# Value spreads cut in halves, three turns of positions moved into a loop, and one key spread moved two steps, in an eight-layer kernel

## What is computed

```python
pe = pos_emb.reshape(Sq, Sq, NH, DH)
k_hop = jnp.einsum('bhvc,vmhc->bhvm', qh, pe)
qk = jnp.einsum('bhsd,bhtd->bhst', qh, k_scaled)
C = (qk + k_hop) * D
```

## Time and profile before

| | us |
|---|---|
| three runs | 758.37, 757.95, 753.97 |
| median | 757.95 |
| the profiled execution | 758.14 |
| span of its trace | 756.3 |
| busy: PE, PEld, DVE, ACT, POOL | 655.7, 451.2, 572.8, 525.6, 319.4 |
| mean granted clock of TensorE | 0.947 |

### The profile page before, as it was taken

One profiled execution on the slowest core, in us unless ns is written; L12 is line 12 of the kernel. 1 busy time (PEld: TensorE's weight loads), 2 busy tenths in 40 slices (PEclk: granted clock), 3 DMA queues, 4 the chain that ended last, 5 costly groups with the idle time before them and its releaser, 6 DMA issues.

```text
span 756.3 us, 13768 instructions
## 1 busy us (share of the span) xinstructions
PE 655.7 (87%) x5031; PEld 451.2 (60%) x5039; DVE 572.8 (76%) x1105; ACT 525.6 (70%) x1074; POOL 319.4 (42%) x337
## 2 busy tenths in 40 slices
PE   6288999488997998998799999988999998888967
PEld 5167887233554554655795666546888686666622
DVE  5869997887898857998565888668973346666777
ACT  4775663567885764677438776747885689999877
POOL 4776675787766778881000000189930040000000
PEclk8579999799999999999799999989999999999998
DMA  8526482111110114410000000700000000000001
GB/s 301 173 57 181 130 136 70 49 45 35 38 38 25 33 51 76 66 38 12 1 1 1 0 1 1 281 2 1 2 1 1 1 1 1 1 0 1 1 0 55
DMA packets 40273, 36.11 MB, mean 48 GB/s; under 512 B 21800, under 2 KB 30256, under 8 KB 40208
## 3 DMA queue, kind: packets, MB, share of 16 engines
q1 hardware_dynamic: 33616, 21.73, 9.8%
q0 software_dynamic: 6592, 13.51, 7.6%
HBM read 30.11 MB, written 5.11 MB: 47 GB/s over the span
## 4 chain that ended last, share of the span: by engine, by line
PE 57%; DVE 19%; ACT 13%; issue 4%; DMA 3%; POOL 3%; SPq 0%; ACTq 0%; DVEq 0%; POOLq 0%
PE ps L1351 5%; PE ps L1567 4%; PE ps L1604 3%; PE ps L2073 3%; PE ps L1002 3%; PE ps L2337 3%; PE ps L2024 3%; PE ps L1595 3%; PE ps L213 2%; ACT big L2393 2%; PE ps L1585 2%; POOL pe L400 2%; PE ps L217 2%; PE ps L1031 2%; PE ps L1516 2%
## 5 line engine op out<-in xcount | busy, mean ns | idle before, releaser
L1497 POOL DMA_INDIRECT pe<-in_rpe,idx x128 | 135.0, 1055 | 35.7 <-issue 24.5
L1963 POOL TENSOR_SCALAR big<-big,wcols 128x256 f32<-128x256 f32 x1 | 0.9, 937 | 138.9 <-DMA big<-in_l3f_w 138.9
L384 POOL DMA_INDIRECT pe<-normed_rows,pe x46 | 48.6, 1057 | 20.2 <-issue 10.1
L525 ACT ACTIVATE pe<-ps,wcols 128x256 f32<-128x256 f32 x92 | 38.5, 476 | 22.4 <-PE ps L432 22.4
L1707 ACT ACTIVATE big<-ps,small 128x128 f32<-128x128 f32 x128 | 34.7, 382 | 17.5 <-PE ps L1595 17.5
L1212 ACT ACTIVATE big<-ps 128x1024 f32<-128x1024 f32 x32 | 32.6, 1019 | 18.1 <-PE ps L999 17.9
L1351 PE MATMUL ps<-nT,big 128*128 128x512 f16 x192 | 44.5, 379 | 0.0
L432 PE MATMUL ps<-big 128*128 128x256 f16 x276 | 36.8, 287 | 5.6 <-DVE big L578 4.4
L2337 PEld LDWEIGHTS ps<-big,pe 128*128 128x128 f32 x288 | 34.3, 192 | 11.9 <-ACT big L2385 5.9
L1232 DVE TENSOR_REDUCE small<-ps 128x16 f32<-128x1024 f32 x32 | 38.3, 1216 | 1.5 <-PE ps L993 1.5
L2337 PE MATMUL ps<-big,pe 128*128 128x128 f32 x288 | 35.5, 277 | 1.8 <-ACT big L2385 1.8
(11 more groups left out here) (429 smaller groups left out, 1971.2 us busy)
## 6 DMA issues: line engine op xcount, KB each, us to landing
pe<-in_l2f_w SPq DMA_DIRECT2D x16, 256.0 KB, 6.1
tile_results<-big SPq DMA_DIRECT2D x23, 128.0 KB, 2.2
pe<-in_xrow SPq DMA_DIRECT2D x4, 512.0 KB, 5.3
big<-in_l0x_w SPq DMA_DIRECT2D x8, 256.0 KB, 7.0
pe<-in_rpe,idx POOLq DMA_INDIRECT x128
cT<-in_cT SPq DMA_DIRECT2D x2, 512.0 KB, 4.6
nT<-in_l0x_w SPq DMA_DIRECT2D x4, 256.0 KB, 7.7
vx<-in_l0x_w SPq DMA_DIRECT2D x4, 256.0 KB
```

The costliest lines, as they stand in the source:

```text
L384: pool.indirect_dma_start(out=xg16[:, i % RX, h, :, :].rearrange("p r n -> p (r n)"), out_offset=None, in_=xrows_d, in_offset=bass.Indirec ...
L525: ins_ = act.activation(hid32[:, i % RF, f, :], hidden_ps(i, u)[:, f % 2, :], ACT.Relu, bias=wcols[:, bass.ds(at + (COL_AT["l0x_b1"][0] + ...
L1497: pool.indirect_dma_start(out=pe[:, v * D:(v + 1) * D], out_offset=None, in_=ins["rpe"], in_offset=bass.IndirectOffsetOnAxis(ap=idx[:, v:v ...
```

## The change

1. GpSimd's first key spread (batch 13) moves from step 8 to step 6: `KEYS_IN = (6, 9, 10)`.
2. In layer 3 the last step (k = 15) has no turn between selectors and components any more; its three turns come after the components, on TensorE and on Scalar (`between(k)`).
3. Spreads of chunks 1, 2 and 3 are cut into two halves: positions 0 to 63 (u = 0) and 64 to 127 (u = 1) of each batch. Before the hop loop only the first halves are made. The second halves of chunk 1 are GpSimd's, eight instructions behind its last gather (`pool_rest4`). Those of chunks 2 and 3 are made inside the hop loop: two by Vector after each of f = 0, 2, ..., 10, one by Scalar after each of f = 1, 3, 5, 9. TensorE waits for all 24 of them at f = 16.
4. Vector norms chunk 2, spreads its halves, and only then norms chunk 3.
5. Turns 29, 30 and 31 leave the head and go into the hop loop, at f = 7, 11 and 15, on TensorE and on Scalar.

```diff
-        POOL_KEYS, KEYS_IN = range(13, B), (8, 9, 10)
+        POOL_KEYS, KEYS_IN = range(13, B), (6, 9, 10)
...
+        def between(k):
+            return 13 <= k < NC * NCH // 2 - 1
...
-                    if done == "sel" and k >= 13:
+                    if done == "sel" and between(k):
                         pe_turn_positions(te, first_turn(k))
...
-                if k >= 13:
+                if between(k):
                     act_turned(act, first_turn(k))
...
+        def half4(c, h, u):
+            vs = slice(u * S // 2, (u + 1) * S // 2)
+            return (qblk[:, c * BC:(c + 1) * BC, vs, h], nT[:, cs(c)].rearrange("p (b v) -> p b v", b=BC)[:, :, vs],
+                    hm8[:, h:h + 1])
...
+        def dve_half4(dve, c, h, u):
+            dve.tensor_scalar(*half4(c, h, u), None, MUL).then_inc(s_rest4 if u else X4["qblk"], 1)
+
+        def pool_rest4(pool):
+            pool.wait_ge(s_norm, 2 * NCH + 2)
+            for h in range(NH2):
+                pool.tensor_scalar(*half4(1, h, 1), None, MUL).then_inc(s_rest4, 1)
...
+        LATE_TURNS = (7, 11, 15)
...
-            pe_turn_positions(te, PG - 3)
-            pe_turn_positions(te, PG - 2)
             pe_gates4(te, 1)
-            pe_turn_positions(te, PG - 1)
             pe_gates4(te, 2)
             pe_gates4(te, 3)
-            te.wait_ge(X4["peT_act"], PG)
+            te.wait_ge(X4["peT_act"], PG - 3)
             te.wait_ge(X4["qblk"], NH2 * NCH)
             for f in range(PG):
+                if f in LATE_TURNS:
+                    pe_turn_positions(te, PG - 3 + LATE_TURNS.index(f))
+                if f == PG // 2:
+                    te.wait_ge(s_rest4, REST_0 + NH2 * (NCH - 1))
+                if f >= PG - 3:
+                    te.wait_ge(X4["peT_act"], f + 1)
...
-            for g in range(PG - 3, PG):
-                act_turned(act, g)
             for c in (2, 3):
                 act.wait_ge(s_norm, 2 * NCH + c + 1)
                 for h in (6, 7):
-                    act_spread4(act, c, h)
+                    act_half4(act, c, h, 0)
...
+                if f in LATE_TURNS:
+                    act_turned(act, PG - 3 + LATE_TURNS.index(f))
+                if f in (1, 3, 5, 9):
+                    n = (1, 3, 5, 9).index(f)
+                    act_half4(act, 2 + n // 2, 6 + n % 2, 1)
...
             for h in range(NH2):
-                dve_spread4(dve, 1, h)
-            dve_normed(dve, 4, 2, bank(4))
-            dve_normed(dve, 4, 3, bank(5))
+                dve_half4(dve, 1, h, 0)
             for c in (2, 3):
+                dve_normed(dve, 4, c, bank(2 + c))
                 dve.wait_ge(s_norm, 2 * NCH + c + 1)
                 for h in range(6):
-                    dve_spread4(dve, c, h)
+                    dve_half4(dve, c, h, 0)
...
                 dve.tensor_copy(*khop_group(f)).then_inc(X4["khop_dve"], 1)
+                if f < 12:
+                    for n in (f, f + 1):
+                        dve_half4(dve, 2 + n // 6, n % 6, 1)
...
             if stop > 2:
                 pool_layer2(pool, link)
+            if stop > 4:
+                pool_rest4(pool)
```

More of the change, by code:

```diff
@@ L1364, in pe_layer3 @@
                         te.wait_ge(s_norm, 2 * NCH)
-                    for g in range(first_turn(k) + (k >= 13), first_turn(k + 1)):
+                    for g in range(first_turn(k) + between(k), first_turn(k + 1)):
                         pe_turn_positions(te, g)
@@ L1403, in act_turned, with act_half4 @@
             act.activation(*turned(g), ACT.Copy).then_inc(X4["peT_act"], 1)
+        s_rest4, REST_0 = F1["up"], FT * NCH
         def spread4(c, h):
-            return qblk[:, c * BC:(c + 1) * BC, :, h].rearrange("p b v -> p (b v)")
-        def act_spread4(act, c, h):
-            act.activation(spread4(c, h), nT[:, cs(c)], ACT.Copy, scale=hm8[:, h:h + 1]).then_inc(X4["qblk"], 1)
-        def dve_spread4(dve, c, h):
-            dve.tensor_scalar(spread4(c, h), nT[:, cs(c)], hm8[:, h:h + 1], None, MUL).then_inc(X4["qblk"], 1)
+            return qblk[:, c * BC:(c + 1) * BC, :, h].rearrange("p b v -> p (b v)"), nT[:, cs(c)], hm8[:, h:h + 1]
+        def half4(c, h, u):
+            vs = slice(u * S // 2, (u + 1) * S // 2)
+            return (qblk[:, c * BC:(c + 1) * BC, vs, h], nT[:, cs(c)].rearrange("p (b v) -> p b v", b=BC)[:, :, vs],
+                    hm8[:, h:h + 1])
+        def act_spread4(act, c, h):
+            dst, src, mask = spread4(c, h)
+            act.activation(dst, src, ACT.Copy, scale=mask).then_inc(X4["qblk"], 1)
+        def act_half4(act, c, h, u):
+            dst, src, mask = half4(c, h, u)
+            act.activation(dst, src, ACT.Copy, scale=mask).then_inc(s_rest4 if u else X4["qblk"], 1)
+        def dve_spread4(dve, c, h):
+            dve.tensor_scalar(*spread4(c, h), None, MUL).then_inc(X4["qblk"], 1)
+        def dve_half4(dve, c, h, u):
[4 more added lines that the diff above has]
+                pool.tensor_scalar(*half4(1, h, 1), None, MUL).then_inc(s_rest4, 1)
         def dve_layer3(dve, link):
```

## The result

| | before | after |
|---|---|---|
| median of 19 runs, us | 758.09 | 753.03 |
| lowest and highest, us | 753.35 to 760.14 | 747.69 to 755.97 |
| ratio (95% interval) | | 0.9931 (0.9914 to 0.9948) |
| profiled execution, us | 758.14 | 754.47 |
| span of its trace, us | 756.3 | 752.6 |

5.1 us less by the medians, where 4.0 were forecast. The sum was nearly right; its terms were not. Lines of the code have moved: layer 3's products are L1354, turns L1539, full and half spreads of Vector L1427 and L1430, GpSimd's halves L1435, hop products L1594, the first score products behind the loop L1612 (L1585 before), L1443 is L1466, L1448 is L1471.

What follows compares the result with a forecast made beforehand. No engine bounds the whole span; Vector bounds layer 3's head, TensorE the hop loop. Terms -3.4 - 1.9 + 1.3 = -4.0 us against 758.14 gave 754.1, stated as 754.0; 8 in 10 between 749.5 and 759.

Steps and rivals of the forecast that it cites:

- Part 1: Layer 2, key spread in step 6 instead of 8: L1304 freed, taken -3.4 us, bounds -1.2 and -4.7.
- the new meeting: Step 9: batch 14's key spread holds up Vector's L1301, which ends at 240.7 instead of 238.8.
- the late form of part 1: Query spread follows in step 9 without a gap, perhaps low clock; step 10 at 244.0, gain as low as 1.2 us.
- Part 1's reason: Step 9: L1301, issued 0.1 us ahead of the key spread, loses as L1304 did with 0.63 us.
- The new place in step 6: Key spread starts at 220.4, L1301 ends at 220.23: 0.2 us of air, nothing counted, small chance of a 3 us stall.
- Part 2: Layer 3, step 15: four transposes of 0.44 us leave the way of the last components; xT earlier, taken -0.4 us.
- Part 3: Head, spreads by halves at 0.35 us each: loop starts at 364.4 instead of 366.3, -1.9 us including the earlier xT.
- the alternation: Layer 3's end and head: GpSimd's halves and Vector take turns; L1448 waits 0.9 us twice, L1412 0.9 each; chance 0.45.
- The example at 501: L2213, issued at 501.43 inside the first of two 1.16 us GpSimd instructions, ended at 502.51 between them.
- Part 4: Hop loop: three turns on TensorE at 0.44 us each, taken +1.3 us, bounds +1.3 and +1.8.
- The whole stop of Vector: Rival: GpSimd's eight halves in a row hold Vector before the hop loop; total about 758, up to 761.3 us; chance 0.13.
- The second, no new meeting: Rival, step 9: L1301 gets through first, sum -5.3 to -6.9, 751 to 753 us; chance 0.25.

Runs made afterwards that it cites:

- the run without the meeting: Changed kernel with the key spreads in steps 7, 10 and 11 instead of 6, 9 and 10: 749.29 us, ratio 0.9871.
- turns in the wait: Changed kernel with key spreads in steps 7, 10 and 11 and turns 29 and 30 between gate products of chunks 2 and 3: 748.48 us, ratio 0.9849.
- the memset: Changed kernel with a 0.22 us GpSimd memset between the last gather and each of the three key spreads: 748.27 us, ratio 0.9847.
- the run with the turns back: Changed kernel with turns 29 to 31 moved from the hop loop back into the head: 750.23 us, ratio 0.9863.

## Why the prediction was right, and where its terms were not

**Part 1, the gain and the new meeting: right.** Forecast -3.4 up to step 10, measured -3.4. L1301 was to take 2 to 3 us and took 2.58; TensorE was to wait 2 to 3 us before step 10 and waited 2.02. The low clock behind it was left for the late form of part 1; it came in the changed kernel's profile behind 2.02, took 1.6 us, and did not come in the four other profiles on the first two chips with this wait (2.01 three times, 2.02 once). What decides isn't shown. The query spread followed without a gap, as the late form had feared, and cost Vector nothing, because L1301 came in first.

**Part 1's reason: right in its assumption, now with a test.** I took L1301 to lose although it is issued first. It lost with 0.11 us of lead behind a gather, and won with 0.39 and 0.20 behind a memset. The literal reading of the Trainium skill's page "SBUF — State Buffer" ("Who interferes with whom": whoever issues first keeps the ports) would have given -4.7, and the run without the meeting shows what that would have been worth: 1.5 us more. If the hold begins during the gather, the page's sentence and the rows agree again, and the recorded start is not the moment of the issue. That reading fits all meetings here, but where the hold begins isn't measured.

**The new place in step 6: right.** 0.2 us of air was enough. L1301 there has 0.68 us.

**Part 2, -0.4: mis-sized.** The first half of xT is done 0.4 us earlier, as forecast: at 349.37, and layer 3 starts 0.9 us earlier here, so this is 350.3 in the count of the kernel before, which had 350.70. But the step "the three turns then lie in the 2.66 idle us before L213" was costed at nothing, and it is worth more than the 0.44: with turn 26 at 347.71 the idle before L213 is 1.17 us, the clock stays up, and L213 takes 1.96 instead of 3.03 us, the two turns behind it 0.87 instead of 1.48 on the chain. Undone alone, the edit costs 1.5 us up to the loop's start.

**Part 3, -1.9 with part 2: the step that failed is the alternation.** L1448 was to wait twice 0.9 us and L1412 twice; they waited not at all, and GpSimd waited up to 4.3 us for them. The example at 501 was the other case, a Vector instruction that comes while a GpSimd one is running and has gaps before it; Vector's instructions here follow each other with none. The price is 0.6 us in one block of this profile, and nothing in eight others. The prediction's own sum was off here too: the waits that it lists on L1448 and L1412 add up to 3.6 us, and it moved Vector's end of chunk 1 by 2.8 (355.7 to 358.5). With 3.6 parts 2 and 3 would have come to -1.1 and the whole to -3.2. Halves cost 0.29 to 0.30, between the bound of 0.26 and the 0.35 taken, which over the twenty on Vector's way is 1.1 us. Undisturbed I had 362.8 - 366.3 = -3.5 for parts 2 and 3; the marks show -5.2 (77.9 to 72.7 us from layer 3's first product to the loop), and -5.7 in five profiles without the 0.6. The clock of part 2 (1.7) and the cheaper halves make up the difference: Scalar had the norm of chunk 2 ready so early that only 0.2 us of Vector's time was lost waiting for it. The loop's start is then set by the last gate products, at clock 0.50 until 360.20, 0.1 us behind Vector's last half.

**Part 4, +1.3: the turns cost it, the loop doesn't lose it all.** On the chain each turn in the loop has 0.44 us. From the first hop product to the first score products (L1585, now L1612) it takes 34.7 us instead of 34.0: +0.7, since full clock is back 4.5 us after the start (364.7) and not 5.7 us. Vector and Scalar have room: the copies of the first f still end ahead of f+3.

```profile
368.87 0.44 PE ps L1539 x4
369.31 0.89 PE ps L1594 x8
```

**The rivals.** The whole stop of Vector didn't happen. The second, no new meeting, is seen in three experiments on the first two chips (spreads in 7, 10 and 11, turns in the wait, the memset) and is 1.5 us better, or 3.1 where the clock would fall.

**The sum: luck in good part.** The terms as measured are -3.4, -5.2 and +0.7, together -7.9, twice the forecast. In the profiled pair 1.6 us of low clock behind the second meeting, 0.9 ahead of layer 2 and 1.7 in the rest bring this back to -3.7. None of the three stands in the forecast's sum. By the medians 5.1 are left.

## What to carry to other kernels

A GpSimd instruction that reads SBUF must be laid out against Vector's instructions with two SBUF operands, with the gather in front of it counted in: moving it away from one meeting can put it into the next, and a memset of 0.22 us in front of it was as good as a better step on the second chip (layer 2 took 100.8 us either way). It is no cure by itself: in the kernel before, on the third chip, the key spread behind the memset stopped the next Vector instruction instead. Small work of TensorE belongs in its waits, and it isn't enough to take it off the path: two turns put into an idle stretch gave 0.9 us themselves, and the stretch gained 1.4 more with the clock, in one profile. Where an edit saves a few microseconds, compare stretches between marks in the traces, and look whether a stretch without an edit moves with it; the rest, which no edit touches, took 352.4 to 357.8 us here, with the clock.

## What the runs showed of the hardware that I had not expected

- The meeting of GpSimd and Vector goes either way. A key spread behind a gather stopped a Vector instruction issued 0.11 and 0.63 us ahead of it; behind a memset it waited for one issued 0.20 and 0.39 us ahead; a row of Vector instructions without gaps held a GpSimd half for 4.3 us (5.52 instead of 1.17 to 1.20), and did so in seven profiles (5.50 to 5.62). In the two profiles in which the halves were through before that row began, none took over 2.44.
- Spreads with a distance of eight elements in the output: on GpSimd 256 elements take 1.17 us where a plain 128x256 took 0.94. On Vector 256 take 0.29 and 512 take 0.51 us, on Scalar some 0.6 (1.25 for two) and 1.03.
- The clock fell behind a wait of 2.02 us in one kernel and stayed up behind 2.01 and 2.02 in four others with the same steps around it. With 1.12 to 1.20 us before L213 it stayed up in nine profiles, the changed kernel's among them, and with 1.15 us in the run with the turns back it was at 0.50 from 349 to 352 us.
